# Latent attention of a two-layer kernel: scores computed a second time in transposed form, in place of transposed probabilities, and folded projection weights

## What is computed

```
h = rmsnorm(x) * g1;   c = h @ w_down                 # 256 -> 128
q, k = rope(c @ wq), rope(c @ wk);  v = c @ wv        # 16 heads of 8
scores = q k^T / sqrt(8), causal;  attn = softmax(scores)
x = x + (attn v) @ w_up                               # 128 -> 256
t = rmsnorm(x) * g2;   probs = softmax(t @ router_w)  # 8 experts, top 2
x = x + gated sum of the 2 experts' FFNs of t
```

## Time and profile before

| | us |
|---|---|
| runs | 939.69, 939.76, 940.22; median 939.76 |
| span of the profiled execution | 950.8 |
| latent stage in it, to the last `cnt` | 0 to 223.6 |
| first token rows loaded for the experts | issued at 229.96 |

### The profile page before, as it was taken

One profiled execution on the slowest core, in us unless ns is written; L12 is line 12 of the kernel. 1 busy time (PEld: TensorE's weight loads), 2 busy tenths in 40 slices (PEclk: granted clock), 3 DMA queues, 4 the chain that ended last, 5 costly groups with the idle time before them and its releaser, 6 DMA issues.

```text
span 950.8 us, 24923 instructions
## 1 busy us (share of the span) xinstructions
PE 898.3 (94%) x8496; PEld 805.4 (85%) x8496; DVE 715.1 (75%) x1942; ACT 608.7 (64%) x1694; POOL 293.8 (31%) x359
## 2 busy tenths in 40 slices
PE   5899999887999999999799999999999999999997
PEld 4676677554999999999689898888988989999996
DVE  5768898755666666766889887997878737888867
ACT  4477778763666666666587665866877326677740
POOL 4736665634000000001533434342112102445430
PEclk9999999988999999999999999999999999999999
DMA  8239200062111111133010022021005952333335
GB/s 315 101 112 434 100 23 25 24 245 72 46 51 55 48 56 51 51 135 128 23 35 27 25 87 88 24 89 50 14 20 207 402 141 84 93 100 96 96 106 206
DMA packets 43037, 97.23 MB, mean 102 GB/s; under 512 B 6080, under 2 KB 28480, under 8 KB 41504
## 3 DMA queue, kind: packets, MB, share of 16 engines
q1 hardware_dynamic: 36048, 76.83, 23.1%
q0 software_dynamic: 6864, 18.80, 5.8%
HBM read 62.24 MB, written 33.37 MB: 101 GB/s over the span
## 4 chain that ended last, share of the span: by engine, by line
PE 79%; DVE 10%; DMA 4%; issue 3%; ACT 2%; POOL 1%; another core or an unknown queue 1%; SPq 0%; DVEq 0%; ACTq 0%; POOLq 0%
PE ps L893 23%; PE ps L722 10%; PE ps L724 9%; PE ps L723 9%; PE ps L980 3%; PE ps L990 3%; PE ps L1004 3%; PE ps L815 2%; PE ps L1062 2%; PE ps L829 2%; PE ps L788 2%; PE ps L868 1%; DMA CT<-in_ctxT 1%; DMA BIG<-ys_dram,YI 1%; PE ps L878 1%
## 5 line engine op out<-in xcount | busy, mean ns | idle before, releaser
L722 PE MATMUL ps<-BIGR 128*128 128x256 f32 (+1 forms) x826 | 258.6, 313 | 4.0 <-DVE BIGR L1707 1.0
L893 PE MATMUL ps<-BIG 128*128 128x128 f32 x2000 | 250.7, 275 | 1.1 <-issue 1.0
L893 PEld LDWEIGHTS ps<-BIG 128*128 128x128 f32 x2000 | 237.2, 192 | 1.6 <-issue 1.2
L724 PE MATMUL ps<-BIGR 128*128 128x256 f32 x778 | 221.2, 284 | 0.0
L723 PE MATMUL ps<-BIGR 128*128 128x256 f32 (+1 forms) x602 | 177.1, 294 | 0.0
L722 PEld LDWEIGHTS ps<-BIGR 128*128 128x128 f32 x826 | 157.0, 190 | 12.2 <-issue 6.2
L724 PEld LDWEIGHTS ps<-BIGR 128*128 128x128 f32 x778 | 147.4, 189 | 0.7
L1202 ACT COPY BIG<-BIG 128x512 f32 (+1 forms) x86 | 70.1, 815 | 101.4 <-PE ps L893 78.9
L723 PEld LDWEIGHTS ps<-BIGR 128*128 128x128 f32 x602 | 114.8, 191 | 1.7
L1680 DVE TENSOR_TENSOR BIGR<-BIG,BIGR 128x512 fp32r<-128x512 f32 (+1 forms) x86 | 80.9, 940 | 35.6 <-ACT BIGR L1211 34.9
L1952 POOL DMA_INDIRECT BIG<-ys_dram,YI x32 | 34.8, 1087 | 224.3 <-DMA ys_dram<-BIG 216.0
(11 more groups left out here) (234 smaller groups left out, 1878.1 us busy)
## 6 DMA issues: line engine op xcount, KB each, us to landing
BIG<-in_wgu SPq DMA_DIRECT2D x2, 6144.0 KB
BIG<-in_wd SPq DMA_DIRECT2D x2, 4096.0 KB
BIG<-xs_dram SPq DMA_DIRECT2D x47, 129.5 KB
xs_dram<-CT SPq DMA_DIRECT2D x8, 640.0 KB
BIG<-xs_dram SPq DMA_DIRECT2D x39, 128.0 KB
ys_dram<-BIG SPq DMA_DIRECT2D x39, 128.0 KB, 1.7
BIG<-in_wkv SPq DMA_DIRECT2D x2, 2048.0 KB, 8.9
kv_dram<-BIG SPq DMA_DIRECT2D x16, 256.0 KB, 2.0
```

Source lines behind the costliest of these rows:

```text
L722: pe.matmul(o, l[0], r[0], start=start, stop=False)
L724: return pe.matmul(o, l[1], r[0], start=False, stop=stop)
L893: i = pe.matmul(o[:, c * 128:(c + 1) * 128], wt[:, at:at + 128], x[:, k * 128:(k + 1) * 128], start=k == 0, stop=k == 1)
```

## The change

1. `c` and `c_e` go. The weights are folded once at the start: `foldT` transposes w_down and w_up, `fold` multiplies w_down by (wq, wk, wv), and w_up by the router's weights, `fold_e` copies them out. `qkv` is then two matmuls of 392 columns that read the transposed 256 features directly; its last 8 columns are the router logits of the normed input.
2. `tT`, `tT_e` and `log` go. `wup` has 264 columns, the last 8 being the router's share of the attention output, and `r` adds the two parts of the logits along with the residual. `ra` reads the logits from SBUF.
3. `s` is ordered by tile and its masks are made in tiles of 32 by 64 (20 small bf16 matmuls; before 8 in tiles of 64 by 64). It now serves only the maxima; a `max` frees its bank.
4. New: `nm` (DVE, two small instructions) writes the negated maxima as a bf16 high part and a bf16 remainder; `mT` (PE) transposes them with one matmul, `mT_e` (ACT) copies them out. `st` (PE) computes the scores again with keys on partitions: 8 fp32 matmuls, 4 bf16 matmuls for the empty corner, 32 bf16 matmuls of 128 or 64 columns that add the negated maxima in PSUM, 16 for the masks. `qkh` makes the masked queries it needs: four more ACT multiplications of 128 columns.
5. `exp` is four activations of 512 columns, PSUM to SBUF, already in the layout that `pv` reads. `pT` and `pT_e` go.
6. `pv` has 16 matmuls: the values have a column of ones beside them. Its output has the sums in other rows, so `onrm` transposes 256 columns in blocks of 32 on DVE, takes the reciprocal of 16 columns, multiplies twice (64 columns each) and transposes 128 columns back.
7. `rope` is one addition over 256 columns, since the sine has its sign in a constant. The conversion of places to integers moves from `rb` (DVE) to a new ACT phase `pi`, in both layers.
8. The ring "s" has banks 0 to 5, for `s` and `st` both. The probabilities have eight buffers in place of four. `LEAD` and the costs have new values for the latent phases; the planner adds 60 to 170 ns where PE changes its tile shape. `ch` in layer 1 also waits for the keys of an earlier group.

```diff
-for _name, _n in (("ident", 128), ..., ("neg", 128), ("rc", 8), ("rs", 4),
+for _name, _n in (("ident", 128), ..., ("neg", 64), ("negt", 64), ("sel", 4), ("rc", 8), ("rs", 4), ("rsn", 4),
...
+            if engine == "PE" and TILING.get(k[0], "whole") != tiling:
+                t = max(ready[k], clock.get(engine, 0.0) + 110) + 60
...
-RINGS = {"misc": (4, 5, 6, 7), "s": (0, 1, 2, 3), "pT": (4, 5, 6, 7), "pv": (4, 5, 6, 7),
+RINGS = {"misc": (4, 5, 6, 7), "s": (0, 1, 2, 3, 4, 5), "pv": (4, 5, 6, 7),
...
+            def fold():
+                for k in range(2):
+                    i = pe.matmul(ps("fold", i=k)[:, 0:384], wT[:, k * 128:k * 128 + 128], wqkv, start=True, stop=True)
...
             def qkv(b):
-                pe.matmul(ps("qkv", b)[:, 0:384], cT_[b % 2], wqkv, start=True, stop=True).then_inc(*fills("qkv", b))
+                for k in range(2):
+                    i = pe.matmul(o, hnT_[b % 2][:, k * 128:k * 128 + 128], WQ_[:, k, :], start=k == 0, stop=k == 1)
...
+            def mT(b):
+                pe.wait_ge(*done("nm", b))
+                pe.matmul(ps("mT", b)[:, 0:128], nm_[b % 2], identb, start=True, stop=True).then_inc(*fills("mT", b))
+            def st(b):
+                pe.wait_ge(*emptied("mT", b))
+                for h in range(2):
+                    for g, at in enumerate(strips):
+                        pe.matmul(o[h][g][:, :, 64 * h:128], k[at, 64 * h:64 * h + 64], q[at, :, 64 * h:128],
+                                  start=True, stop=False)
+                for g, at in enumerate(strips):
+                    pe.matmul(o[1][g][:, :, 0:64], onesb[at, 0:64], mask(at, 63, 64).broadcast_to([32, 4, 64]), ...)
+                for n in range(4):
+                    for h in range(2):
+                        for g, at in enumerate(strips):
+                            pe.matmul(o[h][g][:, n, 64 * h:128], selb[at, n, :], nmt_[b % 2][at, 64 * h:128], ...)
+                for h in range(2):
+                    for x in range(2):
+                        for g, at in enumerate(strips):
+                            i = pe.matmul(o[h][g][:, :, 64 * h:64 * h + n], identw[at, lo:lo + 64], early, ...)
...
             def exp(b, g):
-                for n in range(4):
-                    i = act.activation(p_[g][:, at], ps("s", b, i=g)[:, at], ACT.Exp, bias=sm[:, 4 * g + n:4 * g + n + 1])
-            def pT_e(b, g):
-                act.copy(pt_[g], ps(f"pT{g}", b)[:, :]).then_inc(*frees(f"pT{g}", b))
+                act.activation(pt_[4 * (b % 2) + g], ps("st", b, i=g)[:, :], ACT.Exp).then_inc(*frees("st", b, i=g))
...
+            def nm(b):
+                v.tensor_copy(o[:, :, 0:4], m).then_inc(dv, next_step("dve"))
+                then()
+                v.tensor_tensor(o[:, :, 4:8], m, o[:, :, 0:4], ALU.subtract).then_inc(S["negmax"], 1)
             def nrm0(b):
-                v.reciprocal(o, ps("pv", b)[:, 128:256]).then_inc(dv, next_step("dve"))
-                v.tensor_tensor(o, ps("pv", b)[:, 0:128], o, ALU.mult).then_inc(*frees("pv", b))
+                v.transpose(ot_, ps("pv", b)[:, 0:256]).then_inc(*frees("pv", b))
+                v.reciprocal(sr_..., sums[:, :, 16:18])
+                for x in range(2):
+                    v.tensor_tensor(on_..., sums[:, at, 0:16]..., sr_..., ALU.mult)
+                v.transpose(oT_[b % 2], on_).then_inc(S["heads_normed"], 1)
```

More of the change, by code:

```diff
@@ L215, in latent_phases @@
-        add("PE", 1800, ("pv", b), *[(f"pT_e{g}", b) for g in range(4)], banks=[("pv", ("onrm", b))])
-        add("DVE", 1250, ("onrm", b), ("pv", b), ("wup", b - 2))
+            add("DVE", 680, (f"max{g}", b), ("s", b))
+        add("DVE", 250, ("nm", b), *[(f"max{g}", b) for g in range(4)], ("mT", b - 2))
+        add("PE", 60, ("mT", b), ("nm", b), banks=[(misc, ("mT_e", b))])
+        add("ACT", 220, ("mT_e", b), ("mT", b), ("st", b - 2))
+        add("PE", 1250, ("st", b), ("mT_e", b), ("qkh", b), banks=[("s", (f"exp{g}", b)) for g in range(4)])
@@ L221, in latent_phases @@
+        add("ACT", 520, ("sq", b), ("r", b), ("eps3", b - 6))
+        add("DVE", 140, ("eps3", b), ("sq", b))
         add("POOL", 550, ("pow3", b), ("eps3", b))
-        add("DVE", 420, ("tt", b), ("pow3", b), ("sc", 0, b - 3))
-        add("POOL", 750, ("xr", b), ("r", b))
-        add("PE", 220, ("tT", b), ("r", b), ("log", b - 2), banks=[(misc, ("tT_e", b))])
-        add("ACT", 300, ("tT_e", b), ("tT", b), ("log", b - 2))
-        add("PE", 450, ("log", b), ("tT_e", b), banks=[(misc, ("ra", 0, b))])
@@ L227, in latent_phases @@
-        add("DVE", 800, ("ra", 0, b), ("log", b), ("cnt", b - 2), ("rb", 0, b - 4))
+        add("DVE", 550, ("tt", b), ("pow3", b), ("sc", 0, b - 3))
+        add("POOL", 725, ("xr", b), ("r", b))
+        add("DVE", 850, ("ra", 0, b), ("r", b), ("cnt", b - 2), ("rb", 0, b - 4))
         add("PE", 130, ("cnt", b), ("ra", 0, b), banks=[(misc, ("rb", 0, b))])
-        add("DVE", 850, ("rb", 0, b), ("cnt", b))
-        add("POOL", 2550, ("sc", 0, b), ("rb", 0, b), ("tt", b), *[("fill",) for _ in range(b == FILLED)], late=2000)
+        add("DVE", 750, ("rb", 0, b), ("cnt", b))
@@ L232, in latent_phases @@
+        add("ACT", 200, ("pi", 0, b), ("rb", 0, b))
+        add("POOL", 2350, ("sc", 0, b), ("pi", 0, b), ("tt", b), *[("fill",) for _ in range(b == FILLED)], late=2000)
     for u in range(4):
@@ L783, in s @@
                 q, k = qkt_[b % 2], km_[b % 2].rearrange("p (n t) -> p n t", n=4)
-                for half, keys, masked_too in ((0, slice(0, 128), True), (1, slice(0, 64), False), (1, slice(64, 128), True)):
-                    for g in range(4):
-                        at, rows = slice(32 * g, 32 * g + 32), slice(64 * half, 64 * half + 64)
-                        o = ps("s", b, i=g)[rows, :].rearrange("p (n t) -> p n t", n=4)
-                        pe.matmul(o[:, :, keys], q[at, rows], k[at, :, keys], start=True, stop=not masked_too)
```

441 lines of the change are left out of this document (247 added, 194 removed), and 13 rows, old and new, of the table LEAD.

## The result

The changed kernel takes 954.27 us (median of 4, 953.77 to 955.84) against 939.74 of the kernel before (4 runs, 939.69 to 940.22): a ratio of 1.0152, with a 95% interval of 1.0135 to 1.0169. It is 14.5 us slower where 13 us less were forecast. The execution profiled took 953.99 us with a span of 951.8.

The account below looks back on a forecast made before the run. PE was taken as the bound of the latent stage, DVE close behind. Savings of 8.8 us (middle), 2 (start) and 2.3 (end) made 13.1; 13 off 939.76 gave 926.8 us, forecast 919 to 935, wider range 909 to 944.

Parts of the forecast that it names:

- PE was to give back 1.2 us a batch: PE in the latent stage: 3.71 us removed, 2.5 added, from 9.9 to 8.7 us a batch.
- D: Latent stage: clock at half for a tenth of it, 937 us; chance 0.10 together with C and mild A.
- DVE was to stay as it was: DVE in the latent stage: 1.97 us added against 1.93 removed a batch, so nothing.
- The failed step: Middle of the latent stage: DVE at 95% gives 9.7 us a batch, 0.8 less, 8.8 us over 11 batches.
- A second step: Whole kernel: runs 1.2% below the profiled span counted as error, so 13 us came off the median of 939.76.
- The rival of 915 to 919 us: Stage end: a better order avoids DVE's 4.7 us outside wait and late scatters, 8 to 12 us more; chance 0.12.
- The start: Before 58 us: two batches' worth of PE work gets shorter, 2 us; the fold costed at nothing.
- The end: From 174 us on: four batches save 4.8 us, the last batch's longer way takes 2.5 back; 2.3 us less.
- In layer 1 nothing, within 1 us: Layer 1: the integer conversion moves off DVE, which is no bound there; no effect, within 1 us.
- B: PE stands before mT and st until the maxima are through: slower, 959 us at 2.4 uncovered; nearly all of 0.18.
- A: Latent stage: DVE and the longer way keep the period near 10.4 us, 936 us; mild form shares 0.10.
- C: Small matmuls of st and s cost the high end, PE gives back 0.3 us a batch, 937 us; shares 0.10.

Follow-up runs that it names:

- h0: The kernel before, unchanged, run once more for a profile that belongs to 940 us: 939.86 us, span 938.0.
- f4: The changed kernel with the kernel before's table of due times, new phases' entries as after: 993.31 us, ratio 1.0565 to the kernel before.
- i1: The changed kernel with the planner's costs taken from traces and a table of due times searched anew: 942.75 us, ratio 1.0026 to the kernel before.
- i2: The kernel before with the folded weights, the two small reliefs of DVE and a newly searched table of due times: 952.5 us, ratio 1.0134.
- h2: The kernel before, no instruction changed, only the planner's costs of rope and rb 100 ns lower each: 951.21 us, ratio 1.0116.
- g1: The kernel before with one rope instruction for two and the integer conversion on ACT, planner's costs adjusted: 952.89 us, ratio 1.0122.
- f2: The kernel before with the folded weights alone, scores and probabilities as before: 943.19 us, ratio 1.0024.
- e1: The kernel before, unchanged, profiled once more: 953.67 us, ratio 0.9988, span 955.0.
- f5: The changed kernel without nm, mT and mT_e, st reading a table of zeros for the maxima: 946.06 us, ratio 1.0069 to the kernel before.
- e4: The changed kernel with fill started behind batch 9 in place of 11: ratio 1.0217 to the kernel before.

## Why the prediction was wrong

**The terms were near, in part by luck.** `st` was taken as 1.75 us. Its timeline:

```profile
141.09 1.09 PE L872 MATMUL ps<-BIG 32*64 32x512 f32 x16 [0.44 <-DVE BIG L1513]
141.60 0.29 PE L875 MATMUL ps<-negb,onesb 32*64 32x256 bf16 x4
141.71 0.88 PE L881 MATMUL ps<-BIG,small 32*64 32x64 bf16 x32
142.39 0.44 PE L889 MATMUL ps<-negt,identw 32*64 32x128 bf16 x16
```

It takes 142.83 - 141.09 = 1.74 us. But its split was off: the fp32 part makes way after 0.51 us, not 1.07, and the small matmuls take 1.2 us, not 0.7. From 141.60 to 142.83 that is 0.024 us each, close to the high end. PE was to give back 1.2 us a batch and gave 19.7 / 16 = 1.2. That agreement is luck in part: much of the changed stage ran at the lower clock level, where the same matmuls are drawn longer (the rows of D, below). Counting what PE did there as half, I estimate about 1.8 us a batch at full clock.

DVE was to stay as it was, and 715.1 us both times looks like it. But behind the stage DVE has 6.1 us less (539.0 for 545.1), since the conversion left layer 1 as well, and in the stage it has more: 176.2 us, against 170.0 in the first profile and 171.6 in h0, some 0.3 us a batch. Its new rows (0 to 237 us):

```profile
L1513 DVE TENSOR_REDUCE BIG<-ps 128x4 f32<-128x512 f32 x64 | 41.0, 680 | 11.9 <-PE ps L846 11.8
...
L1539 DVE TENSOR_TENSOR BIG<-BIG 128x64 f32<-128x64 f32 x32 | 8.5, 305 | 0.6
...
L1533 DVE STREAM_TRANSPOSE BIG<-ps 128x256 f32<-128x256 f32 x16 | 7.0, 440 | 3.6 <-PE ps L906 3.6
...
L1546 DVE STREAM_TRANSPOSE BIG<-BIG 128x128 f32<-128x128 f32 x16 | 5.0, 311 | 0.5
...
L1535 DVE RECIPROCAL BIG<-BIG 128x16 f32<-128x16 f32 x16 | 4.0, 253 | 0.5
```

The transposes were priced 0.42 and 0.29 and are 0.44 and 0.31; of the new instructions only the products came out dearer, 0.305 for 0.23. Some that the change does not touch last longer, too: the comparison that makes the one-hot rows takes 304 ns for 189. ACT fell by 3.1 us a batch for the forecast's 3.4.

**The failed step is the one from work to period:** "with DVE held at 95% a batch takes 9.2 / 0.95 = 9.7 us". It carried 8.8 of the 13.1 us. It supposes that one engine can be kept full. Here five engines run lists whose order is fixed before the start; each batch goes back and forth between PE, DVE, ACT and POOL many times; the change adds three crossings (`nm`, `mT`, `mT_e`) and makes all four exponentials wait for all four maxima. How full an engine gets is then a property of the order: the same instructions take 10.7 us a batch as the change stands (from `pv` of batch 0 to that of batch 15), 12.7 with the old table (f4, 69.6 to 259.7 us), 9.9 with the one of i1. In 68 to 164 us DVE was at 82% in the change, not at 95%. Nor did the step hold with the better order: in i1 DVE is at 87%, as in the kernel before, and 9.2 / 0.87 = 10.6 us is the period that i1 has over its first eleven batches. The fullest that any profile shows DVE in that stretch is i2 with 87.0 of 96 us, 91%, and its batches are 10.7 us apart; so nothing here supports 95, and a fuller DVE was no shorter period. h2 puts a price on the order: 11 us for a disturbance in the plan alone, nearly as much as the whole gain forecast.

**A second step failed, and it was passed over in one sentence:** "The runs lie 1.2% below the span; so much is within the error of the sum". 1.2% is 11 us. h0 shows that it was 9.7 us at the end of the stage and 3.1 behind it. The rival of 915 to 919 us and part of the credit for the end rested on a wait that h0, whose time is that of the timed runs, doesn't have.

**The start** gave more than the "2 us": `pv` of batch 0 began 7.5 us earlier than in h0 (2.1 us in i1). **The end** did not give back 2.3 us: from `pv` of batch 11 to the first expert rows it is 229.74 - 179.68 = 50.1 us, in h0 220.28 - 172.66 = 47.6. **"In layer 1 nothing, within 1 us"** came out as some 4: 722.1 us behind the stage against 717.7. i1 still has 2.7 of these. It may be the conversion on ACT: g1, which has it and not the added wait of `ch`, needs 721.9, and f2, which has neither, 718.7. But it stays open, for the profiles scatter as much: f4 has both edits and needs 718.0, and the kernel before needs 720.8 in its first profile and 724.7 in e1.

**The rivals.** B had the sign, and 959 was nearer than 926.8. Its mechanism may be part of the matter: with the trip gone, and the order changed with it, the kernel is 8.4 us faster (f5). But the rows above give `st` and `mT` 4.3 us of waits for `L1513` and `L1528` in 100 us, some 0.5 a batch, where B said "from 1.2 us uncovered a batch on, the gain is gone"; the rest of the gaps stood before other phases, and stayed when the trip went. A ("DVE and the longer way cover the gain: the period stays near 10.4", 936 us) had the middle of i1 right, 10.6 us with DVE at 87%; it had the change as it stands wrong. C was wrong in effect (`st` is as long as forecast).

D needs its rows. Stretches of the changed kernel at the lower clock level from 100 us on (busy PE, clock, DMA share, GB/s):

```profile
119.90:123.30 3.40, 3.38 (x75) 0.50 1.10 475
147.20:150.60 3.40, 3.40 (x80) 0.50 0.02 5
164.30:167.70 3.40, 3.40 (x67) 0.50 0.02 5
177.90:181.30 3.40, 3.40 (x98) 0.50 0.01 2
195.00:198.40 3.40, 3.40 (x66) 0.50 0.51 208
212.10:225.80 13.70, 8.11 (x29) 0.50 0.22 78
sum 30.70, PE 25.09; mean PE 4.18
```

At 0.50, that is 1.2 GHz, PE does in 25.1 us what would take 12.5 at the full level; h0 has one such stretch in the stage, 6.8 us long with PE busy for 4.8. (The change and i1 have one more each at about 15 to 25 us, before the first `qkv`; h0 has none there.) The Trainium skill describes the pattern in "TensorE: Matmul & The Clock Gate", section "A second HAM failure mode: psum-queue depth-cycling": a PE that idles briefly and often between groups of matmuls swings between its two levels; the trace agrees, with PE standing for 23.9 us in 100 here and 7.5 in h0. It would be easy to put the 14.5 us down to it. i1 speaks against that:

```profile
sum 23.80, PE 20.92 PEld 11.94 DVE 15.70 ACT 7.52 POOL 11.52; mean PE 4.18 PEld 2.39 DVE 3.14 ACT 1.50 POOL 2.30
```

It has 23.8 us at the lower level with PE busy for 20.9 of them, 10.5 us lost by the same count, and PE stands for 24.7 in 100, and its latent stage is shorter than that of the kernel before. So at least that much at the lower level can be had without a longer stage. That it falls off the path there, and on it in the change, is argued and not shown. How much of the 14.5 us it was in the change could not be separated, since no experiment held the clock up.

What is settled: with another order of the same instructions the change costs 2.9 us and not 14.5; the difference, 11 to 12 us, is order. What is not: why the one order is that much better than the other, since the plan has them 0.5 us apart. Wrong costs account for 9.5 us of the plan's own error (-3.7 to +5.8), and nothing accounts for the other 9 of the 14.5. And no version found beats the kernel before, so whether the work that PE saves in each batch can be turned into time is open; A's reason against it, DVE with some 9 us a batch that no order filled to 95%, is not refuted.

## What to carry to other kernels

Where a fixed order has been fitted to a kernel, an edit changes two things, the work and the fit, and the second can be larger than the first: change a cost that only the planner reads, and see how far the time moves, before any saving below that is believed or blamed. Give the planner the durations of the new phases from a trace (one wrong by 450 ns a batch moved the planned end by some 6 us), and don't judge an edit by one order alone; but measure the new order too, for a planned end is no proof: of two found by the plan, i1 gained 11 us and i2 came out 12.7 us behind the kernel before. Don't forecast an engine fuller than any trace has shown it in that kernel. And when the profile at hand is a per cent away from the timed runs, find out in which stage it differs before a forecast of one per cent is read from it.

## What the runs showed of the hardware that was not expected

- Small matmuls in different tiles of PE start close together: L881 starts at 141.71 and L889, 32 matmuls later, at 142.39, 21 ns each. The Trainium skill, "TensorE: Matmul & The Clock Gate", section "Wait — 56ns, not 53.3ns?", gives about 25 ns as the least distance of two starts. The measurement decides: in tiles of 32 by 64 it is less, if not by much.
- The 16 records of the fp32 part of `st` are drawn as 1.09 us, but the next group starts 0.51 us after they do.
- A block transpose on DVE costs what another instruction of its size does: 440 ns for 128 by 256 out of PSUM (a sum of that size takes 416), 311 ns for 128 by 128 (the product of the kernel before takes 291).
- Two profiles of the kernel before, with spans of 938.0 and 950.8 us, are alike to within 0.4 us up to batch 11. The longer one then has two waits of DVE, 2.4 and 4.7 us long, for something outside the engines, and a stretch of 6.8 us at the lower clock level behind them. Such waits stand in the profiles of `before` and e1 to e4 and in no other; what they are for, no run shows.
- A short stretch at the lower clock level shows nothing of the gaps that came before it: in four of the six above PE is drawn as busy through all of it (3.40 of 3.40 us).
